# Result rows of expert slots: four homes chosen by the kind of slot, in place of two

## The chip, the cores and the metric

The kernel runs on one core of one Trainium2 chip. The metric is the device time of one execution in microseconds (us), as the median of several runs.

## What is computed

The input is 8 sequences of 512 rows of 256 numbers (4096 tokens). The reference adds three things: the input, a gated linear scan along each sequence, and a mixture of experts on the normalised rows. The change is in the last one:

```python
scores = jax.nn.sigmoid(xf @ Wg.T + bg + bias)
top_scores, top_idx = jax.lax.top_k(scores, TOP_K)      # 2 of 8 experts for each token
h = jax.nn.gelu(jnp.einsum('td,ehd->teh', xf, W1) + b1, approximate=False)   # 256 -> 1024
eo = jnp.einsum('teh,edh->ted', h, W2) + b2                                  # 1024 -> 256
combined = jnp.einsum('ted,te->td', eo, weights)
shared = jax.nn.gelu(xf @ Ws1.T + bs1, approximate=False) @ Ws2.T + bs2
```

The kernel computes an expert only for the tokens that chose it: 8192 pairs of token and expert, sorted into lists.

## The kernel before

**Two parts.** The first part runs over the 8 sequences: projections, scan, shared expert, routing, and the store of a base result to `out`. It ends near 275 us. The second part works through 43 slots. A slot is a run of list entries that belong to one expert, of 256 rows (28 of them, "large"), 128 rows (8) or 64 rows (7). The tables of constants fix the order: slots 0 to 13 are large, slot 14 has 128 rows, then come six blocks of large, 64-row, large, 128-row (slots 15 to 38), and at the end large, large, 64-row, 128-row (39 to 42). `order(n)` (line 89) makes the description of slot n. `s.u` is n modulo 2, `s.c` is n modulo 4, `s.kth` counts the slots of the same size before it, `s.added` is the value of the semaphore `add_out[s.u]` once all adds of the slots of this parity up to n have landed. `ahead(n, c)` (line 84) is the same for large slots inside a hardware loop, where n is a register's value.

**A slot's way through the engines.** The order is written out by hand, engine by engine.
- SP loads the slot's list of rows, its list of places and weights (`slot_adds`), its parameters and its second bias row. `adds_list(s, s2)` waits until the adds of slot n-2 have landed, then loads the list of slot n+2 (line 380). SP also copies 1 MB of weights for each 64-row slot (line 423), since those slots keep their weights apart.
- POOL gathers the rows from memory by index (line 557), four slots ahead.
- PE turns the rows (line 1375). In a large slot it turns those of slot n+2 at its fifth step, in a 128-row slot at its first one. Then it runs the first layer (lines 1297 for large, 1333 for small slots) three steps ahead of the second layer (1305, 1356).
- ACT applies the gelu (line 656), DVE splits the result into a high and a low half-precision part (lines 930 and 931), and PE's second layer reads these.
- In slot n DVE also writes, into the home of the slot's result, the weighted bias rows (`bias_rows`, line 1159, its instruction at 1168): in a large slot behind the sixth of eight splits, in a small slot behind the fourth of four. In slot n+1 DVE adds the weighted PSUM result to that home (`result`, line 1175, its instruction at 1188). For a 64-row slot the result is turned back in between.
- POOL then adds the home's rows to `out` by index (`scatter_add`, line 561, its instruction at 570), one DMA per 128-row tile. It first waits for the adds of slot n-1 to land, because two slots can add to the same row of `out`.

**The homes.** `y_sb` (line 182) has two homes of 512 columns in the scratch tile `arena`, used in turn by s.u. Before it writes bias rows, DVE waits until the home is free, which is when the adds of slot n-2 have landed:

```python
if not isinstance(s.n, int) or s.n >= 2:
    dve.wait_ge(add_out[s.u], s.added - 16 * s.tiles)
    dve.wait_ge(y_ok, s.n + S_A + 1)
```

Columns 4096 to 5120 of `arena` hold the base result of a sequence in the first part. In the second part 4096 to 4608 hold two of the four bias rows, and 4608 to 5120 are unused.

Of the kernel before, what the change touches and what calls it, by code (L numbers as in the profile page):

```python
# [29 lines left out]
ALU, ACT, AX = mybir.AluOpType, mybir.ActivationFunctionType, mybir.AxisListType  # L30
# [3 lines left out]
SEQS, SEQ, D, H, E = 8, 512, 256, 1024, 8  # L34
# [3 lines left out]
ROWS, MID, LOW = 256, 128, 64  # L38
NA, NB, NC = 28, 8, 7
SLOTS = NA + NB + NC  # L40
FIRST = NA // 2
# [20 lines left out]
EV_A, H_A, S_A = SEQS * EVENTS, SEQS * KH, 2 * SEQS  # L62
# [26 lines left out]
def order(n):  # L89

    if not 0 <= n < SLOTS:
        return None
    past = SIZES[:n]
    dmas = [16 * max(r // P, 1) for r in SIZES[:n + 1]]
    return Slot(n, n, SIZES[n], past.count(SIZES[n]), sum(UNITS[r] for r in past), sum(dmas[n % DEEP::DEEP]),
                sum(dmas[n % 2::2]))


class Tally:


# [22 lines left out]
def layer(nc, x, w1, w2, gates, b1, b2, gbias, sbias, out):  # L124
    ctx = ExitStack()
    with ctx:
        def sb(name, shape, dt):
            return ctx.enter_context(nc.sbuf_tensor(name, shape, dt))

        def sem(name):  # L130
            return ctx.enter_context(nc.semaphore(name))
# [12 lines left out]
        arena = sb("arena", [P, 7680], F32)  # L144
# [34 lines left out]
        spare = arena[:, 0:512].bitcast(U32)  # L179
        zeros = arena[:, 512:1024]  # L180
        b2rows = [b2row[0], b2row[1], arena[:, 4096:4096 + D], arena[:, 4096 + D:4096 + 2 * D]]
        y_sb = [arena[:, 2048 + i * 512:2560 + i * 512] for i in range(2)]
        low_w1, low_w2, mid_w1 = (h[:, :].bitcast(F16) for h in (stage[0], stage[1], arena[:, 5120:7168]))
        late = arena[:, 7168 + KD * LOW:7168 + KD * LOW + 256]
        factors = [small[:, 200 + 2 * i:202 + 2 * i] for i in range(2)]
# [91 lines left out]
        hhl_ok, y_ps, y_ok = sem("hhl_ok"), sem("y_ps"), sem("y_ok")  # L277
# [12 lines left out]
        add_out = [sem(f"add_out{i}") for i in range(2)]  # L290
# [173 lines left out]
        def _(pool):  # L464
            own = Tally(pool, pool_own)
# [95 lines left out]
            def scatter_add(s):  # L561

                if s.n:
                    pool.wait_ge(add_out[1 - s.u], order(s.n - 1).added)
                for t in range(s.tiles):
                    if t < s.tiles - 1:
                        pool.wait_ge(add_ok, s.kth + 1)
                    else:
                        pool.wait_ge(y_ok, S_A + s.n + 1 + 2)
                    pool.indirect_dma_start(  # L570
                        out, bass.IndirectOffsetOnAxis(ap=slot_adds[s.c][0:s.parts, t, 0:1], axis=0),
                        y_sb[s.u][0:s.parts, t * D:(t + 1) * D], None, compute_op=ALU.add).then_inc(add_out[s.u], 16)

            pool.wait_ge(xhl_out, 16 * SEQS)
            pool.wait_ge(ev_ps, EVENTS * (SEQS - 1))
# [2 lines left out]
            for n in range(SLOTS):  # L578
                if n + DEEP < SLOTS:
                    gather(order(n + DEEP))  # L580
                if n == 0:
                    pool.wait_ge(o_out, 16 * SEQS)
                scatter_add(order(n))
# [214 lines left out]
        def _(dve):  # L798
            own = Tally(dve, dve_own)
            V = nc.vector  # L800
# [358 lines left out]
            def bias_rows(s):  # L1159

                dve.wait_ge(b2_in[s.c], (s.n - s.c) * 4 + 16)
                dve.wait_ge(adds_list_in[s.c], (s.n - s.c) * 4 + 16)
                if not isinstance(s.n, int) or s.n >= 2:
                    dve.wait_ge(add_out[s.u], s.added - 16 * s.tiles)
                    dve.wait_ge(y_ok, s.n + S_A + 1)
                r, weight = s.parts, slot_adds[s.c][:, :, :].bitcast(F32)
                for t in range(s.tiles):
                    own.mark(V.scalar_tensor_tensor(out=y_sb[s.u][0:r, t * D:(t + 1) * D], in0=b2rows[s.c][0:r, :],
                                                    scalar=weight[0:r, t, 1:2], in1=bs2[0:r, :], op0=ALU.mult,
                                                    op1=ALU.add))  # L1170
                if s.rows != LOW:
                    own.mark(V.tensor_scalar(factors[s.u][:, 0:s.tiles], weight[:, 0:s.tiles, 1], par[s.c][:, 2:3], None,
                                             ALU.mult))

            def result(s):

                if s.rows == LOW:
                    dve.wait_ge(yT_ps, s.kth + 1)
                else:
                    dve.wait_ge(y_ps, s.unit + s.units + H_A + RING)  # L1180
                own.settle()
                for t in range(s.tiles):
                    r, c = s.parts, slice(t * D, (t + 1) * D)
                    if s.rows == LOW:
                        src, factor = ps_l[0:r, 0:D], slot_adds[s.c][0:r, 0, 1:2].bitcast(F32)
                    else:
                        src, factor = ps_y[s.u][:, c], factors[s.u][:, t:t + 1]
                    V.scalar_tensor_tensor(out=y_sb[s.u][0:r, c], in0=src, scalar=factor, in1=y_sb[s.u][0:r, c],  # L1188
                                           op0=ALU.mult, op1=ALU.add).then_inc(add_ok if t < s.tiles - 1 else y_ok, 1)

            def slot(s, back, late=(), first=False):

                for j in range(KH):
                    split_h(s, j, first)
                    if j == 0 and back is not None and back.rows == LOW:
                        turn(back)
                    if j == 1 and back is not None and back.rows != LOW:
                        result(back)
                    if j == 2 and back is not None and back.rows == LOW:
                        result(back)  # L1200
                    if j in late:
                        late_tables(late[j])
                    if j == 5:
                        bias_rows(s)

            def small_slot(s, back):

                for k in range(s.units):
                    split_h(s, k)
                    if k == 0 and back.rows == LOW:  # L1210
                        turn(back)
                    if k == 1:
                        result(back)
                    if k == 3:
                        bias_rows(s)
# [299 lines left out]
```

## Time and profile before

| | us |
|---|---|
| median of 3 runs (lowest, highest) | 672.48 (672.28, 672.95) |
| the profiled execution, its own time | 667.34 |
| its span, first to last instruction | 665.2 |
| mean granted clock of TensorE | 0.997 of full |

The profile shows one execution. PE is TensorE's matmuls, DVE VectorE, ACT ScalarE, POOL GpSimd, SP SyncE. "idle before <-releaser" is the time in which an engine stood before an instruction, and what ended that wait. A pair such as "arena L1168 <- DMA out" means: line 1168, which writes the arena, waited for a DMA that writes `out`. Busy time of a matmul is modelled, and some matmul records can be missing.

### The profile page before, as it was taken

How to read it: one execution, taken by the hardware profiler on the slowest of the kernel's cores; microseconds unless marked ns; L12 is line 12 of the kernel's file. 1: busy time of each engine (PE TensorE's matmuls, PEld its weight loads, DVE VectorE, ACT ScalarE, POOL GpSimd, SP SyncE). 2: the span in 40 equal slices, each digit the busy share in tenths (PEclk: the TensorE clock that was granted, in tenths of full speed). 3: DMA queues.
4: the chain of work that ended last, by engine and by line, in shares of the span. 5: the costliest groups of instructions: out<-in, count | busy, mean ns of one | idle time of the engine just before them, and what ended most of it. 6: DMA issues, size and time to landing. Idle time of an engine off the chain costs nothing.

```text
span 665.2 us, 19468 instructions
## 1 busy us (share of the span) xinstructions
PE 633.9 (95%) x6090; PEld 499.6 (75%) x6091; DVE 535.0 (80%) x1422; ACT 413.7 (62%) x703; POOL 279.3 (42%) x263
## 2 busy tenths in 40 slices
PE   4799999999999999999999999999999999999994
PEld 3365757575656665788888888999989998989883
DVE  4889898999999989887767677777777877787774
ACT  6997886969696966444445444556555554555552
POOL 3132323324242535345454545344545554545423
PEclk9999999999999999999999999999999999999998
DMA  7516345352526142333333254445656665666622
GB/s 243 211 40 184 96 128 112 111 138 83 168 75 199 33 100 68 106 75 59 64 53 68 49 127 116 121 112 138 188 162 161 186 152 167 168 162 192 189 40 29
DMA packets 69455, 81.02 MB, mean 122 GB/s; under 512 B 25684, under 2 KB 61460, under 8 KB 66568
## 3 DMA queue, kind: packets, MB, share of 16 engines
q1 hardware_dynamic: 54264, 62.35, 30.3%
q0 software_dynamic: 15120, 17.77, 15.4%
q8 instruction: 39, 0.64, 0.4%
q14 instruction: 32, 0.26, 0.2%
HBM read 38.66 MB, written 18.10 MB: 85 GB/s over the span
## 4 chain that ended last, share of the span: by engine, by line
PE 77%; DVE 8%; issue 5%; DMA 4%; ACT 3%; POOL 1%; POOLq 0%; SPq 0%; DVEq 0%; ACTq 0%
PE bank L1305 29%; PE bank L1297 29%; PE bank L1285 7%; PE bank L1356 4%; PE bank L1333 4%; DMA out<-arena,slot_adds 3%; PE bank L1375 2%; DVE arena L931 1%; DVE arena L930 1%; DVE W L837 1%; PE bank L1276 1%; DMA arena<-in_gates 1%; PE bank L1241 1%; ACT arena L656 1%; POOL out L570 1%
## 5 line engine op out<-in xcount | busy, mean ns | idle before, releaser
L1305 PE MATMUL bank<-W,arena 128*128 (+1 forms) x2112 | 276.9, 273 | 8.4 <-DVE arena L931 8.4
L1297 PE MATMUL bank<-rows,W 128*128 128x256 f16 (+1 forms) x1728 | 272.6, 296 | 2.3 <-issue 1.1
L656 ACT ACTIVATE arena<-bank,par 128x256 f32<-128x256 f32 (+2 forms) x344 | 169.6, 518 | 147.5 <-PE bank L1297 126.1
L1305 PEld LDWEIGHTS bank<-W,arena 128*128 128x128 f16 x2112 | 201.3, 98 | 44.8 <-issue 8.3
L1297 PEld LDWEIGHTS bank<-rows,W 128*128 (+1 forms) x1728 | 164.5, 98 | 56.5 <-issue 4.7
L570 POOL DMA_INDIRECT out<-arena,slot_adds x71 | 117.7, 1658 | 139.9 <-DVE arena L1188 76.3
L930 DVE TENSOR_SCALAR arena<-arena,par 128x256 f16<-128x256 f32 (+1 forms) x284 | 101.5, 357 | 52.3 <-ACT arena L656 47.4
L931 DVE SCALAR_TENSOR_TENSOR arena<-arena,par 128x256 f16<-128x256 f32 (+1 forms) x284 | 134.0, 472 | 10.0
L508 POOL DMA_INDIRECT lists<-entry,place x64 | 69.4, 1084 | 119.0 <-ACT arena L638 64.6
L1285 PE MATMUL bank<-rows,W 128*128 128x512 f16 x288 | 63.7, 379 | 0.0
L662 ACT ACTIVATE rows<-bank 128x1024 f16<-128x1024 f16 (+2 forms) x43 | 36.1, 840 | 36.3 <-PE bank L1375 35.9
L645 ACT ACTIVATE arena<-bank,PT 128x512 f32<-128x512 f32 x64 | 49.3, 772 | 10.2 <-DVE arena L931 10.2
L638 ACT ACTIVATE arena<-bank,small 128x512 f32<-128x512 f32 x48 | 36.6, 771 | 26.4 <-PE bank L1285 26.0
L557 POOL DMA_INDIRECT arena<-xhl_rows,slot_rows x34 | 34.8, 1023 | 40.4 <-ACT arena L656 34.7
L557 POOL DMA_INDIRECT rows<-xhl_rows,slot_rows x37 | 38.4, 1039 | 31.2 <-ACT arena L656 14.8
L1285 PEld LDWEIGHTS bank<-rows,W 128*128 128x128 f16 x288 | 27.5, 98 | 31.6
L931 DVE SCALAR_TENSOR_TENSOR arena<-arena,PT 128x512 f16<-128x512 f32 x64 | 48.2, 753 | 2.3
L837 DVE SCALAR_TENSOR_TENSOR W<-stage,small,W 128x1024 f16<-128x1024 f32 (+1 forms) x32 | 40.0, 1278 | 0.8 <-ACT W L612 0.8
L930 DVE TENSOR_SCALAR arena<-arena,PT 128x512 f16<-128x512 f32 x64 | 31.5, 492 | 8.0 <-PE bank L1305 6.2
L612 ACT ACTIVATE W<-stage,small 128x1024 f32 (+1 forms) x32 | 36.5, 1143 | 0.0
L601 ACT ACTIVATE W<-stage 128x1024 f32 (+1 forms) x32 | 33.5, 1047 | 0.0
L1188 DVE SCALAR_TENSOR_TENSOR arena<-bank,small,arena 128x256 f32<-128x256 f32 x64 | 28.4, 480 | 6.0 <-PE bank L1356 3.6
(186 smaller groups left out, 549.6 us busy)
## 6 DMA issues: line engine op xcount, KB each, us to landing
stage<-in_w SPq DMA_DIRECT2D x32, 512.0 KB, 4.7
stage<-W SPq DMA_DIRECT2D x14, 1024.0 KB, 5.5
arena<-W SPq DMA_DIRECT2D x8, 1024.0 KB, 5.6
arena<-in_x SPq DMA_DIRECT2D x8, 512.0 KB, 5.5
xhl_rows<-W SPq DMA_DIRECT2D x8, 512.0 KB, 4.5
out<-arena SPq DMA_DIRECT2D x8, 512.0 KB, 5.7
b2row<-in_b SPq DMA_DIRECT2D x22, 128.0 KB, 3.4
arena<-in_b SPq DMA_DIRECT2D x21, 128.0 KB, 3.7
```

The lines of the kernel that those rows point to most:

```text
L508: pool.indirect_dma_start(list_dram, bass.IndirectOffsetOnAxis(ap=place[u][:, c:c + 1], axis=0), entry[u][:, 2 * c:2 * c + 2], None).then_ ...
L557: pool.indirect_dma_start(xg[s.c][0:s.parts, t, :], None, xhl_dram, bass.IndirectOffsetOnAxis(ap=slot_rows[s.c][0:s.parts, t, 0:1], axis=0 ...
L570: pool.indirect_dma_start(out, bass.IndirectOffsetOnAxis(ap=slot_adds[s.c][0:s.parts, t, 0:1], axis=0), y_sb[s.u][0:s.parts, t * D:(t + 1) ...
L638: A((sg[ch], tv[ch], dec)[g], ps_e[(2 * u + i) % RING][:, :], ACT.Tanh, bias=sbt[:, 2 * g + ch:2 * g + ch + 1], scale=(a_half, a_gate, a_h ...
L645: A(h32w[i % WIDE], ps_e[(2 * u + PROJ + i) % RING][:, :], ACT.Gelu, bias=PT[:, 0, 4 + i:5 + i], scale=PT[:, 0, 0:1]).then_inc(ev_act, 1)
L656: ins = A(h32[k][:, c], ps_e[k][:, c], ACT.Gelu, bias=p[:, 4 + e * i + jj:5 + e * i + jj], scale=p[:, 0:1])
L837: ins = V.scalar_tensor_tensor(out=W[:, bass.ds(o + HALF, HALF // 2)], in0=landing(n, l)[:, part * HALF // 2:(part + 1) * HALF // 2], scal ...
L930: seq(V.tensor_scalar(hi, v, p[:, 1:2], None, ALU.mult))
L931: V.scalar_tensor_tensor(out=lo, in0=v, scalar=p[:, 1:2], in1=hi, op0=ALU.mult, op1=ALU.subtract).then_inc(hhl_ok, 1)
L1285: ins = T.matmul(ps_e[(2 * u + i) % RING][:, :], gw[:, wp, c, o:o + P], xT[u][:, 2 * xp + c, :], start=n == 0, stop=n == 3 * KD - 1)
L1297: ins = T.matmul(bank_, weights(w, wp * HALF + c * H + j * P, P), rhs[:, 2 * xp + c, :], start=n == 0, stop=n == 3 * KD - 1)
L1305: ins = T.matmul(banks[t // 2][:, (t % 2) * D:(t % 2 + 1) * D], h[:, hp, t * P:(t + 1) * P], weights(w, (2 + wp) * HALF + j * D, D), start ...
```

## The change

Slots below 14 keep the two homes by parity. From slot 14 on, the home goes by the slot's size: large slots have homes 0 and 1 in turn, by their count; 128-row slots have home 2 and 64-row slots home 3, of 256 columns each, at 4608 and 4864 of `arena`. The wait ahead of the bias rows now names the slot that had the same home last (`preceding`).

```diff
@@ -96,6 +96,16 @@
                 sum(dmas[n % 2::2]))
 
 
+def shares(s):
+
+    return s.u if not isinstance(s.n, int) or s.n < FIRST else s.kth % 2 if s.rows == ROWS else 2 + (s.rows == LOW)
+
+
+def preceding(s):
+
+    return next((order(n) for n in range(s.n - 1, -1, -1) if shares(order(n)) == shares(s)), None)
+
+
 class Tally:
 
 
@@ -179,7 +189,7 @@
         spare = arena[:, 0:512].bitcast(U32)
         zeros = arena[:, 512:1024]
         b2rows = [b2row[0], b2row[1], arena[:, 4096:4096 + D], arena[:, 4096 + D:4096 + 2 * D]]
-        y_sb = [arena[:, 2048 + i * 512:2560 + i * 512] for i in range(2)]
+        y_sb = [arena[:, a:b] for a, b in ((2048, 2560), (2560, 3072), (4608, 4608 + D), (4608 + D, 5120))]
         low_w1, low_w2, mid_w1 = (h[:, :].bitcast(F16) for h in (stage[0], stage[1], arena[:, 5120:7168]))
         late = arena[:, 7168 + KD * LOW:7168 + KD * LOW + 256]
         factors = [small[:, 200 + 2 * i:202 + 2 * i] for i in range(2)]
@@ -569,7 +579,7 @@
                         pool.wait_ge(y_ok, S_A + s.n + 1 + 2)
                     pool.indirect_dma_start(
                         out, bass.IndirectOffsetOnAxis(ap=slot_adds[s.c][0:s.parts, t, 0:1], axis=0),
-                        y_sb[s.u][0:s.parts, t * D:(t + 1) * D], None, compute_op=ALU.add).then_inc(add_out[s.u], 16)
+                        y_sb[shares(s)][0:s.parts, t * D:(t + 1) * D], None, compute_op=ALU.add).then_inc(add_out[s.u], 16)
 
             pool.wait_ge(xhl_out, 16 * SEQS)
             pool.wait_ge(ev_ps, EVENTS * (SEQS - 1))
@@ -1160,12 +1170,16 @@
 
                 dve.wait_ge(b2_in[s.c], (s.n - s.c) * 4 + 16)
                 dve.wait_ge(adds_list_in[s.c], (s.n - s.c) * 4 + 16)
-                if not isinstance(s.n, int) or s.n >= 2:
+                if not isinstance(s.n, int):
                     dve.wait_ge(add_out[s.u], s.added - 16 * s.tiles)
                     dve.wait_ge(y_ok, s.n + S_A + 1)
+                elif preceding(s) is not None:
+                    p = preceding(s)
+                    dve.wait_ge(add_out[p.u], p.added)
+                    dve.wait_ge(y_ok, S_A + p.n + 1 + 2)
                 r, weight = s.parts, slot_adds[s.c][:, :, :].bitcast(F32)
                 for t in range(s.tiles):
-                    own.mark(V.scalar_tensor_tensor(out=y_sb[s.u][0:r, t * D:(t + 1) * D], in0=b2rows[s.c][0:r, :],
+                    own.mark(V.scalar_tensor_tensor(out=y_sb[shares(s)][0:r, t * D:(t + 1) * D], in0=b2rows[s.c][0:r, :],
                                                     scalar=weight[0:r, t, 1:2], in1=bs2[0:r, :], op0=ALU.mult,
                                                     op1=ALU.add))
                 if s.rows != LOW:
@@ -1185,7 +1199,7 @@
                         src, factor = ps_l[0:r, 0:D], slot_adds[s.c][0:r, 0, 1:2].bitcast(F32)
                     else:
                         src, factor = ps_y[s.u][:, c], factors[s.u][:, t:t + 1]
-                    V.scalar_tensor_tensor(out=y_sb[s.u][0:r, c], in0=src, scalar=factor, in1=y_sb[s.u][0:r, c],
+                    V.scalar_tensor_tensor(out=y_sb[shares(s)][0:r, c], in0=src, scalar=factor, in1=y_sb[shares(s)][0:r, c],
                                            op0=ALU.mult, op1=ALU.add).then_inc(add_ok if t < s.tiles - 1 else y_ok, 1)
 
             def slot(s, back, late=(), first=False):
```

## Rows read from the trace of the kernel before

**Rows 1.** First part of the page: busy time, share of the span, instructions.

```profile
PE 633.9 (95%) x6090; PEld 499.6 (75%) x6091; DVE 535.0 (80%) x1422; ACT 413.7 (62%) x703; POOL 279.3 (42%) x263
```

**Rows 2.** Waits: us in total, times, longest; the second from 410 us on.

```profile
DVE arena L1168 <- DMA out<-arena,slot_adds: 11.3, 7, 3.0
...
PE bank L1305 <- DVE arena L931: 3.0, 3, 1.5
```

**Rows 3.** Chain that ended last, 470 to 565 us: start, us, what.

```profile
483.95 7.21 DMA out<-arena,slot_adds
...
546.60 8.06 DMA out<-arena,slot_adds
```

**Rows 4.** Timeline, DVE, bias rows that waited: start, us, instruction, idle before.

```profile
459.47 0.88 DVE L1168 SCALAR_TENSOR_TENSOR arena<-b2row,slot_adds,bs 128x256 f32<-128x256 f32 x2 [1.18 <-DMA out<-arena,slot_adds]
...
491.36 0.92 DVE L1168 SCALAR_TENSOR_TENSOR arena<-b2row,slot_adds,bs 128x256 f32<-128x256 f32 x2 [2.20 <-DMA out<-arena,slot_adds]
...
521.79 0.93 DVE L1168 SCALAR_TENSOR_TENSOR arena<-b2row,slot_adds,bs 128x256 f32<-128x256 f32 x2 [0.86 <-DMA out<-arena,slot_adds]
...
537.04 0.93 DVE L1168 SCALAR_TENSOR_TENSOR arena<-arena,slot_adds,bs 128x256 f32<-128x256 f32 x2 [0.26 <-DMA out<-arena,slot_adds]
...
554.85 0.93 DVE L1168 SCALAR_TENSOR_TENSOR arena<-b2row,slot_adds,bs 128x256 f32<-128x256 f32 x2 [3.05 <-DMA out<-arena,slot_adds]
...
585.89 0.93 DVE L1168 SCALAR_TENSOR_TENSOR arena<-b2row,slot_adds,bs 128x256 f32<-128x256 f32 x2 [1.50 <-DMA out<-arena,slot_adds]
...
617.73 0.93 DVE L1168 SCALAR_TENSOR_TENSOR arena<-b2row,slot_adds,bs 128x256 f32<-128x256 f32 x2 [2.26 <-DMA out<-arena,slot_adds]
```

**Rows 5.** Timeline, PE, the row turns in and behind slots 21, 25, 29, 33, 37.

```profile
490.06 0.61 PE L1375 MATMUL bank<-ident,arena 128*128 128x128 f16 x8
...
496.76 0.29 PE L1375 MATMUL bank<-ident,rows 64*128 64x64 f16 x4
...
521.83 0.61 PE L1375 MATMUL bank<-ident,arena 128*128 128x128 f16 x8
...
527.67 0.29 PE L1375 MATMUL bank<-ident,rows 64*128 64x64 f16 x4
...
552.71 0.61 PE L1375 MATMUL bank<-ident,arena 128*128 128x128 f16 x8
...
560.26 0.29 PE L1375 MATMUL bank<-ident,rows 64*128 64x64 f16 x4
...
585.29 0.61 PE L1375 MATMUL bank<-ident,arena 128*128 128x128 f16 x8
...
591.29 0.29 PE L1375 MATMUL bank<-ident,rows 64*128 64x64 f16 x4
...
616.33 0.61 PE L1375 MATMUL bank<-ident,arena 128*128 128x128 f16 x8
...
623.07 0.61 PE L1375 MATMUL bank<-ident,rows 128*128 128x128 f16 x8
```

**Rows 6.** Timeline, SP's and POOL's DMA issues around the stall of slot 29.

```profile
538.19 0.34 SPq L380 DMA_DIRECT2D slot_adds<-lists  x1
...
547.21 0.50 SPq L423 DMA_DIRECT2D stage<-W  x1
...
548.51 0.97 POOL L557 DMA_INDIRECT rows<-xhl_rows,slot_rows  x1 [0.30 <-issue]
...
554.93 1.43 POOL L570 DMA_INDIRECT out<-arena,slot_adds  x1 [5.46 <-DMA out<-arena,slot_adds]
...
560.79 1.03 POOL L557 DMA_INDIRECT rows<-xhl_rows,slot_rows  x1 [3.11 <-ACT arena L656]
```

**Rows 7.** Line 930 on DVE: all of it (ns min/median/max), and one beside POOL.

```profile
L930 DVE TENSOR_SCALAR arena<-arena,par x284: 276/347/672, 274.5 to 655.0; 128x256 f16<-128x256 f32 x128, 128x128 f16<-128x128 f32 x14
...
547.19 0.62 DVE L930 TENSOR_SCALAR arena<-arena,par 128x256 f16<-128x256 f32 x1
```

## The prediction

> **What bounds the kernel now.** I read the page's first part, then the list of waits, then the timelines of DVE and PE from slot 14 on, then those of POOL and SP around one stall. PE is busy for 95% of the span and DVE for 80% [rows 1], so only time in which PE stands still is to be had. In the list of waits the change touches one entry: DVE, ahead of the bias rows of a slot (line 1168), waits seven times for a scatter-add to land, 11.3 us in all [rows 2]. PE is held by DVE's second half of the hidden split (line 931) three times, 3.0 us [rows 2]. The reader should see that these are one story. In the chain of waits two pieces "DMA out<-arena,slot_adds" of 7.21 and 8.06 us stand between a scatter-add's issue and the bias rows [rows 3].
>
> The seven stalls are 1.18, 2.20, 0.86, 0.26, 3.05, 1.50 and 2.26 us [rows 4]. From slot 15 on the slots run in blocks of four (large, 64-row, large, 128-row). Six stalls are in the large slot after a 64-row one (17, 21, 25, 29, 33, 37), because the 64-row slot is short: little time passes between the result of slot n-2 and the bias rows of slot n. The 0.26 is in slot 27.
>
> **What a stall costs PE.** DVE's stall is not PE's loss, so I measured that apart. PE turns the rows of slot n+2 at fixed places of its own program: in the large slot after a 64-row one, ahead of the stall's effect, and at the start of the next (128-row) slot, behind it. The instructions between are the same in every block. The distance is 527.67 - 521.83 = 5.84 us around slot 25; around slot 17 it is the same. It is 496.76 - 490.06 = 6.70, 560.26 - 552.71 = 7.55, 591.29 - 585.29 = 6.00 and 623.07 - 616.33 = 6.74 us around slots 21, 29, 33 and 37 [rows 5]. So PE lost 0.86, 1.71, 0.16 and 0.90 us, in sum 3.63. Against the stalls of the same slots, 2.20, 3.05, 1.50 and 2.26 [rows 4], each loss is the stall less 1.34 to 1.36 us. That is the lead that DVE has over PE at this place; it also says why the stalls of 1.18, 0.86 and 0.26 cost nothing. PE's 3.0 us of idle [rows 2] is most of the 3.63; I take the rest for PE and its feeder ACT getting back into step.
>
> **The change, part by part.**
> 1. *Homes.* From slot 14 on, large slots use homes 0 and 1 in turn by their count, 128-row slots home 2, 64-row slots home 3. Homes 2 and 3 are each one tile of 256 columns at 4608 and 4864 of the arena. That is behind the two bias rows kept at 4096 to 4608, in the space of the shared result, whose store is waited for before the first scatter-add. No instruction is added, and the addresses change no shape: cost nothing.
> 2. *The wait ahead of the bias rows.* Before: all adds of the slots of the same parity up to n-2 have landed. After: those up to the slot that had the same home last, which is n-4 in the blocks (n-3 for slots 15 and 40, n-5 for 41, none for 14 and 16). The adds of n-4 were out before those of n-2 were issued, since POOL waits for each slot's adds ahead of the next slot's. So for slot 29 the new wait was met well before the stall began at 554.85 - 3.05 = 551.80 [rows 4], and all seven stalls go. Behind DVE's wait stood the last splits of the slot, and behind those PE's second layer: this is the 3.63 us.
> 3. *Waits that stay.* The same function waits for the slot's list and bias row. For slot 29 SP issued the list at 538.19 [rows 6], 13.6 us ahead of the time asked. The longest transfer shown took 8.06 us [rows 3], so a list of 2 KB is no new stall: cost nothing. SP still waits for the adds of n-2 before it loads the list of n+2, so SP does not get faster; nor does POOL, whose 64-row add waits 5.46 us for the same landing [rows 6]. These stand still while PE, DVE and ACT move up, by up to 1.71 us a block. What could be late next is behind them on these queues. POOL's gather after that add waits another 3.11 us for ACT [rows 6]: it has that much in hand, more than 1.71. The gather for slot 32 goes out at 548.51 and PE turns it at 560.26 [rows 6, 5], 11.75 us later and 10.0 after the change. Both are covered; cost nothing. If the cover were gone, the price would be at most the 1.71 us again in each block.
> 4. *First fourteen slots.* There the new expression gives the old numbers (n-2): nothing.
> 5. *The end.* From the result of slot 40 on, the last adds follow each other in series; none of the seven waits lies there. The whole end moves up: nothing gained or lost.
>
> Sum: -3.63 us against the profiled execution, 667.34 us with a span of 665.2. The median of the runs is 672.48, 5.14 us more than that execution. I take the same difference from it: 672.48 - 3.63 = 668.85, say **668.8 us**.
>
> The unknown term is how late the adds land where nothing records them. The adds share the DMA engines with a 1 MB copy of weights, issued at 547.21, 0.6 us behind the add of 8.06 us [rows 6, 3]. With every landing 0.5 us earlier PE's losses (stall less 0.5 less 1.34) are 0.36, 1.21 and 0.42, together 2.0. With every landing 0.5 later they are 0.34, 1.36, 0.02, 2.21, 0.66 and 1.42, together 6.0. I take the recorded 3.6 and keep 2.0 to 6.0, that is 666.5 to 670.5.
>
> The row for such a landing is 8.06 us from issue [rows 3]. The Trainium skill, DMA: Bandwidth & Descriptors, section on the anatomy of one DMA on the SWDGE path, fits a transfer as 2.0 us plus its bytes over 436 GB/s: an estimate of 2.3 us for one of these 128 KB adds. By that fit there would be no stall and nothing to gain; the trace disagrees for transfers beside others.
>
> **Rivals.**
> *A, the forecast:* the stalls go, PE gets 3.6 us back. For it: four independent pairs of stall and loss that obey one slack, and lists and gathers with room.
> *B, nothing measurable:* in the timed runs landings come 1 us earlier, so that only slot 29 loses anything (3.05 - 1 - 1.34 = 0.7 us; time 671.8), or a wait that is met at the same landing takes the old one's place (672.5). Against: the runs are slower than the profiled execution, not faster, and no other consumer of that landing is near PE.
> *C, slower:* POOL's issue holds DVE up. During the old stall DVE stood idle exactly while POOL was about to issue the 64-row add (1.43 us) and a gather (1.03) [rows 6]; now DVE works there. If DVE stood for both, it would be 2.46 us in each of the six slots, less 1.34 of lead: 1.12 x 6 = 6.7 us lost where 3.63 were, 672.5 + 3.1 = 675.6. It decides from a hold-up of 1.34 + 3.63/6 = 1.95 us a slot. Against: a DVE split at 547.19, right beside an issue of POOL, took 0.62 us where the median is 0.347 [rows 7]. That is 0.27 us for one instruction, inside the lead even if it happened four times in a block.
> The Trainium skill, SBUF — State Buffer, section Who interferes with whom, has the rule for this: a DVE instruction in a 2-port mode and a GpSimd one exclude each other for the whole instruction. The 0.62 agrees that there is something, not with the full length of POOL's issue.
> *D, more than forecast:* part of the 5.14 us by which the runs exceed the profiled execution are these very stalls. With landings 1 us later the losses are 0.84, 1.86, 0.52, 2.71, 1.16 and 1.92, together 9.0 us: 663.5. Nothing in the trace places the 5.14, so this is open.
> *E, it does not do what it says:* a home shared by mistake would leave a wait on n-2. By the order of sizes each class comes back after four slots, so I give it next to nothing and count it with B.
>
> **How the numbers follow.** A 0.75, D 0.07, B with E 0.13, C 0.05. A measurement of this kernel tells from no change what is over 0.2%, 1.35 us. A from its low bound up and D are faster: 0.82; same 0.13; slower 0.05. The range holds all of A (666.5 to 670.5), part of D below it and the near side of B above it: 665.0 to 671.2.
>
> **What would show it.** In the changed kernel's profile the wait "DVE arena L1168 <- DMA out" (the line moves by some ten) is gone, not moved. The distance from the row turn in slot 29 to the next is 5.84 us, as in all blocks. POOL's waits for landings stay. PE's busy time stays at 634 us while the span falls to about 661.6. I am wrong if DVE waits in the bias rows for a list, if PE shows new waits for gathered rows, if the distances shrink but others grow, or if DVE's splits beside POOL's issues take over 1 us.

## The result and the profile after

| | before | after |
|---|---|---|
| median (lowest to highest), 5 runs each | 672.48 (672.24 to 673.17) | 668.82 (667.78 to 670.13) |
| ratio of the times, 95% interval | | 0.9944 (0.9932 to 0.9955) |
| profiled execution, own time | 667.34 | 668.82 |
| its span | 665.2 | 667.0 |

The changed kernel is 3.7 us faster (672.48 - 668.82), where 3.6 was forecast. The last line of the table is the surprise: by the two profiled spans it would be 1.8 us *slower*. Both readings had to be explained before the forecast could be called right for its reason.

First part of the page of the changed kernel; the engines do the work they did before [rows 1]:

```profile
span 667.0 us, 19466 instructions
## 1 busy us (share of the span) xinstructions
PE 635.1 (95%) x6090; PEld 499.4 (75%) x6091; DVE 534.3 (80%) x1422; ACT 411.1 (62%) x703; POOL 281.7 (42%) x263
```

The wait at the bias rows (now line 1182) is in no list of waits any more, where it stood with 11.3 us [rows 2]. POOL still waits for landings, 44.2 us against 44.9 before, but DVE no longer stands behind these landings. In the chain that ended last, by engine, DMA is down to 1% from 4% before, and no scatter-add's landing [rows 3] is among its costly lines:

```profile
PE 76%; DVE 13%; issue 6%; ACT 3%; DMA 1%; POOLq 0%; DVEq 0%; SPq 0%; POOL 0%; ACTq 0%
```

PE's timeline, the row turns (now line 1389) in and behind slots 21, 25 and 29, to be held against [rows 5]:

```profile
482.11 0.39 PE L1389 MATMUL bank<-ident,arena 128*128 128x128 f16 x4
...
492.77 0.61 PE L1389 MATMUL bank<-ident,arena 128*128 128x128 f16 x8
498.61 0.29 PE L1389 MATMUL bank<-ident,rows 64*128 64x64 f16 x4
...
524.33 0.61 PE L1389 MATMUL bank<-ident,arena 128*128 128x128 f16 x8
530.18 0.29 PE L1389 MATMUL bank<-ident,rows 64*128 64x64 f16 x4
...
545.05 0.39 PE L1389 MATMUL bank<-ident,arena 128*128 128x128 f16 x4
...
555.95 0.61 PE L1389 MATMUL bank<-ident,arena 128*128 128x128 f16 x8
561.79 0.29 PE L1389 MATMUL bank<-ident,rows 64*128 64x64 f16 x4
```

Behind the large slots the distance is 498.61 - 492.77 = 5.84 us, and 5.85 and 5.84 at the next two, where it was 6.70, 5.84 and 7.55. That part came as forecast. But ahead of them, from the turn in the 64-row slot to the one in the large slot, it is 555.95 - 545.05 = 10.90 us, where the kernel before had 10.16. In all six blocks it is 0.50 to 0.78 us above the same distance before. PE's timeline shows why, in the middle of a run of equal matmuls:

```profile
548.09 0.51 PE L1370 MATMUL bank<-arena,stage 128*128 128x64 f16 x10
549.12 0.22 PE L1370 MATMUL bank<-arena,stage 128*128 128x64 f16 x2 [0.53 <-issue]
```

Twelve matmuls that follow each other without any wait on a semaphore are cut after the tenth, by 0.53 us with no releaser ("issue"). Each of the six blocks has such a pause: two inside this third run of twelve, four in the first-layer matmuls (line 1311) right behind it. The profile of before has none. Either the change brings them, or the two profiles come from different circumstances.

Part of the difference of the spans arises ahead of slot 14, from which on the change acts. These are the same row turn in PE's timelines, of the kernel before and of the changed one:

```profile
425.46 0.39 PE L1375 MATMUL bank<-ident,arena 128*128 128x128 f16 x4
```
```profile
427.17 0.39 PE L1389 MATMUL bank<-ident,arena 128*128 128x128 f16 x4
```

Here the second profile is already 1.7 us behind. With 3.8 us more in the six 64-row slots and 3.7 us less at the large slots it ends 1.8 us behind (1.7 + 3.8 - 3.7), which is the difference of the spans. The 1.7 us can't come from the wait that was changed.

### The profile page after: what moved, and what is told of

It reads as the page before. It is cut to its first block, busy times and chain, and to the rows that moved or that the text cites. A ratio compares the mean times of both kernels' runs of the same rounds, so it can differ in the third digit from the quotient of the medians.

```text
span 667.0 us, 19466 instructions
## 1 busy us (share of the span) xinstructions
PE 635.1 (95%) x6090; PEld 499.4 (75%) x6091; DVE 534.3 (80%) x1422; ACT 411.1 (62%) x703; POOL 281.7 (42%) x263
## 4 chain that ended last, share of the span: by engine, by line
PE 76%; DVE 13%; issue 6%; ACT 3%; DMA 1%; POOLq 0%; DVEq 0%; SPq 0%; POOL 0%; ACTq 0%
PE bank L1319 29%; PE bank L1311 28%; PE bank L1299 5%; PE bank L1370 5%; PE bank L1347 5%; PE bank L1389 2%; DVE W L847 2%; DVE arena L941 2%; DVE arena L940 2%; DMA arena<-in_gates 1%; PE bank L1290 1%; DVE arena L880 1%; DVE arena L874 1%; PE bank L1255 1%; ACT W L622 1%
## 5 line engine op out<-in xcount | busy, mean ns | idle before, releaser
L666 ACT ACTIVATE arena<-bank,par 128x256 f32<-128x256 f32 (+2 forms) x344 | 167.7, 518 | 149.9 <-PE bank L1311 126.0
```

Source lines behind the costliest of these rows:

```text
L666: ins = A(h32[k][:, c], ps_e[k][:, c], ACT.Gelu, bias=p[:, 4 + e * i + jj:5 + e * i + jj], scale=p[:, 0:1])
```

## The experiments

Three sets of four kernels. The kernels of a set ran on one chip, and each set on another chip. "Ratio" is to the kernel before on the same chip; its median was 666.43, 673.46 and 666.10 us in the three sets.

### First set: is the gain this wait, and on every chip?

**The kernel before, no edit.** Expected:

> The kernel before, unchanged. Open after the result: its profiled execution took 667.34 us, its timed ones 672.2 to 673.2. Theory A (the seven waits are worth 3.6 us in every execution): median 672.5, and a profile of such an execution shows the distances between row turns around slots 21, 29, 33 and 37 above 5.84 us by 3.6 in sum. Theory D (the shown execution was a lucky one; typical ones lose more to the same waits): the losses sum to 5 to 9 us. Theory F (typical executions lose 3 to 4 us in 64-row slots to pauses of PE that have no releaser, as in the profile of the changed kernel): the distance from the row turn in a 64-row slot to the one in the large slot after it is 10.7 to 10.9 us instead of 10.16.

Measured: 666.56 us, ratio 0.9999 (0.9991 to 1.0008), span 664.2. **The changed kernel, no edit.** Expected:

> The changed kernel, unchanged. All theories: median 668.8, ratio 0.994 to 0.995. A and D: distances of 5.84 us behind the large slots that follow a 64-row one. F: in the 64-row slots 10.7 to 10.9 us again; if they are a property of single executions and not of this kernel, 10.16 can show up.

Measured: 663.23 us, ratio 0.9951 (0.9937 to 0.9965), span 661.3. DVE's bias rows and PE's row turns of the kernel before, on this chip:

```profile
491.47 0.93 DVE L1168 SCALAR_TENSOR_TENSOR arena<-b2row,slot_adds,bs 128x256 f32<-128x256 f32 x2 [2.56 <-DMA out<-arena,slot_adds]
...
522.68 0.93 DVE L1168 SCALAR_TENSOR_TENSOR arena<-b2row,slot_adds,bs 128x256 f32<-128x256 f32 x2 [1.65 <-DMA out<-arena,slot_adds]
```
```profile
489.82 0.61 PE L1375 MATMUL bank<-ident,arena 128*128 128x128 f16 x8
496.88 0.29 PE L1375 MATMUL bank<-ident,rows 64*128 64x64 f16 x4
...
521.95 0.61 PE L1375 MATMUL bank<-ident,arena 128*128 128x128 f16 x8
528.09 0.29 PE L1375 MATMUL bank<-ident,rows 64*128 64x64 f16 x4
```

Slot 21 loses 496.88 - 489.82 - 5.84 = 1.22 us to a stall of 2.56, slot 25 loses 0.30 to one of 1.65: the stall less 1.34 and 1.35. The stalls are not the same ones as in the profile of before (slot 25 had 0.86 and lost nothing), the lead is. Slots 29 and 33 lose 1.09 and 0.45, for stalls of 2.35 and 1.80 (1.26 and 1.35 less). The losses of this execution sum to 1.22 + 0.30 + 1.09 + 0.45 = 3.06 us, and the spans differ by 664.2 - 661.3 = 2.9. The medians differ by 3.2, for about 0.3 us of the gain lies outside the span. In every run of a kernel that has the old wait in all slots, the time is 2.1 to 2.2 us more than the span; in every run of the others it is 1.8 to 1.9 us more. What those 0.3 us are stays open. The changed kernel has 5.84 us at each place and 10.16 to 10.26 in the blocks' other part: no pauses. So the change alone does not bring the pauses.

**Homes without the shorter wait.**

```diff
-                if not isinstance(s.n, int):
+                if not isinstance(s.n, int) or s.n >= 2:
                     dve.wait_ge(add_out[s.u], s.added - 16 * s.tiles)
```

> The four homes with the old wait (the adds of slot n-2). A and D: as slow as before, 672.5, DVE's seven waits are back. A rival by which the addresses or the program's changed layout bring the gain: 668.8.

Measured: 666.62 us, ratio 1.0003 (0.9991 to 1.0014). DVE's waits are back, one of them longer than any seen before:

```profile
618.09 0.93 DVE L1182 SCALAR_TENSOR_TENSOR arena<-b2row,slot_adds,bs 128x256 f32<-128x256 f32 x2 [3.11 <-DMA out<-arena,slot_adds]
```

This stall is in slot 37, and PE lost 1.81 us there; the losses sum to 4.1 us, and the span is 4.1 above the changed kernel's (665.4 - 661.3). The new addresses alone are worth nothing; the wait is everything.

**The old wait in four slots.**

```diff
-                if not isinstance(s.n, int):
+                if not isinstance(s.n, int) or s.n in (21, 29, 33, 37):
                     dve.wait_ge(add_out[s.u], s.added - 16 * s.tiles)
```

> The changed kernel with the old wait put back in slots 21, 29, 33 and 37 alone, those where the stall exceeded DVE's lead of 1.34 us in the profile of before. A: the three relieved stalls (slots 17, 25, 27) were worth nothing, so 672.5 as before. D: typical executions lose in 17 and 25 too, so 671 to 672, between the two kernels.

Measured: 665.82 us, ratio 0.9989 (0.9977 to 1.0002), 0.6 us below before and not clear of it. As a ratio that is where D put it (671 to 672 of 672.5), and the interval just reaches A's 1.0; neither is excluded. Which slots exceed the lead changes from execution to execution, so on this chip slot 25 can be worth something, as the profile of the kernel before had shown (0.30). The four slots of the list carry most of the gain: with them waiting, 2.6 of the 3.2 us are gone again (665.82 - 663.23).

### Second set: how large is the lead, and what part of the change is needed?

**Three homes.** 128-row and 64-row slots share home 2.

```diff
-    return s.u if not isinstance(s.n, int) or s.n < FIRST else s.kth % 2 if s.rows == ROWS else 2 + (s.rows == LOW)
+    return s.u if not isinstance(s.n, int) or s.n < FIRST else s.kth % 2 if s.rows == ROWS else 2
```

> 128-row and 64-row slots share home 2; large slots keep homes 0 and 1 by their count. The small slots then wait again for the adds of slot n-2. A: large slots wait for n-4 still, and no small slot waited in the profile of before, so this is as fast as four homes: ratio to before 0.995. A rival by which each kind needs its own home: back towards 1.0.

Measured: 672.99 us, ratio 0.9986 (0.9970 to 1.0002): not the 0.995. DVE's and POOL's timelines of its end show a term that I had overlooked when I wrote the variant:

```profile
660.15 1.67 POOL L580 DMA_INDIRECT out<-arena,slot_adds  x1 [2.48 <-DMA out<-arena,slot_adds]
...
663.83 0.48 DVE L1182 SCALAR_TENSOR_TENSOR arena<-arena,slot_adds,bs 128x256 f32<-128x256 f32 x1 [3.32 <-DMA out<-arena,slot_adds]
...
665.79 1.56 POOL L580 DMA_INDIRECT out<-arena,slot_adds  x1 [3.98 <-DVE arena L1202]
```

Slots 41 and 42 are the only small slots that are neighbours. Sharing a home, slot 42's bias rows wait for slot 41's add to land, the last add goes out 5.64 us after it in place of 3.49 in the kernel before (659.22 - 655.73), and nothing follows to hide it. Behind the large slots PE kept 5.84 us (5.75 at slot 37). The third set has a variant without this wait, to see whether it was the cause.

This profile shows something else that the account here leaves open. In two of its 64-row slots the distance is 12.26 and 12.24 us, where pauses alone make about 10.9; in both, PE waits 0.98 and 0.92 us for DVE's line 941. The next two variants have two such waits each in these slots (0.30 to 1.07 us). The changed kernel's three profiles and that of the late bias rows below have none. The kernel before has no profile on this chip, so whether it pays this too is not known.

**Three and six more instructions on DVE** ahead of the bias rows of the six large slots that follow a 64-row one, on the changed kernel. They write unused scratch; this is with six (twice three), and three has one round:

```diff
+                if isinstance(s.n, int) and s.n in (17, 21, 25, 29, 33, 37):
+                    for i in range(2):
+                        own.settle()
+                        for to in (rt[:, 0:256], rt[:, 256:512], late):
+                            own.mark(V.scalar_tensor_tensor(out=to, in0=bs2[:, :], scalar=par[s.c][:, 2:3], in1=bs2[:, :],
+                                                            op0=ALU.mult, op1=ALU.add))
```

> Four homes, and ahead of the bias rows of slots 17, 21, 25, 29, 33 and 37 three more VectorE instructions of 256 columns, about 0.40 us apart (0.88 us for two in the profile), so 1.2 to 1.3 us. A (DVE leads PE by about 1.34 us there): no loss, ratio still 0.995; the distances stay at 5.84 us. Rival (no lead, DVE's work counts in full): 6 x 1.25 = 7.5 us more, ratio 1.006.

> The same with six instructions, 2.5 to 2.6 us. A: each of the six slots loses that less 1.34, about 1.2 us, 7 us in all: 4 us slower than before, ratio 1.005 to 1.006. Rival without a lead: 15 us, ratio 1.018.

Measured with three: 670.93 us, ratio 0.9963 (0.9948 to 0.9978), and distances of 5.84 and 5.85 us (5.75 at slot 37). Measured with six: 677.03 us, ratio 1.0049 (1.0031 to 1.0067). DVE's and PE's timelines at slot 21, with six:

```profile
493.64 0.88 DVE L1184 SCALAR_TENSOR_TENSOR rt<-bs,par 128x256 f32<-128x256 f32 x2
494.43 0.48 DVE L1184 SCALAR_TENSOR_TENSOR arena<-bs,par 128x256 f32<-128x256 f32 x1
494.95 0.88 DVE L1184 SCALAR_TENSOR_TENSOR rt<-bs,par 128x256 f32<-128x256 f32 x2
495.75 0.48 DVE L1184 SCALAR_TENSOR_TENSOR arena<-bs,par 128x256 f32<-128x256 f32 x1
496.14 0.88 DVE L1188 SCALAR_TENSOR_TENSOR arena<-b2row,slot_adds,bs 128x256 f32<-128x256 f32 x2
```
```profile
498.07 0.84 PE L1325 MATMUL bank<-W,arena 128*128 x6 [0.95 <-DVE arena L941]
```

The six take 496.14 - 493.64 = 2.50 us. The distance at this slot is 6.98 us, so it loses 1.14, and the lead by this is 1.36; over the six slots it is 1.36 to 1.47. Three take 1.19 us by the same reading and lose nothing. In all six slots the losses are 1.10, 1.14, 1.07, 1.03, 1.03 and 1.05, 6.4 us; the two times differ by 677.03 - 670.93 = 6.1. No DMA plays a part here: the lead is DVE's own, and a held-up DVE costs nearly the same whatever holds it.

**Two homes, bias rows later.** The kernel before with the bias rows of those six slots behind the eighth split.

```diff
-                    if j == 5:
+                    if j == (7 if isinstance(s.n, int) and s.n in (17, 21, 25, 29, 33, 37) else 5):
                         bias_rows(s)
```

> The kernel before, two homes and the old wait, but in slots 17, 21, 25, 29, 33 and 37 the bias rows stand behind the eighth split in place of the sixth, 2.6 us later. A: stalls of up to 2.6 us vanish and 3.05 shrinks to 0.4, so this gets the gain without new homes: ratio 0.995 to 0.996. Rival (the bias rows' own 1.1 us now stand where DVE has less lead, just ahead of the next slot): ratio 0.997 to 1.000.

Measured: 672.18 us, ratio 0.9984 (0.9969 to 0.9999), in the rival's range. Yet its profile looks like A's: two short waits are left (the first is slot 21, the second slot 29), and all distances behind the large slots are unstretched (5.84 or 5.85 us, 5.75 at slot 37).

```profile
494.49 0.92 DVE L1168 SCALAR_TENSOR_TENSOR arena<-b2row,slot_adds,bs 128x256 f32<-128x256 f32 x2 [0.43 <-DMA out<-arena,slot_adds]
...
558.06 0.93 DVE L1168 SCALAR_TENSOR_TENSOR arena<-b2row,slot_adds,bs 128x256 f32<-128x256 f32 x2 [0.78 <-DMA out<-arena,slot_adds]
```

On this chip every one of the four kernels shows the pauses of 64-row slots, this one too, whose instructions on PE are those of the kernel before:

```profile
549.60 0.71 PE L1297 MATMUL bank<-rows,W 128*128 128x256 f16 x5 [0.42 <-issue]
...
581.10 0.19 PE L1356 MATMUL bank<-arena,stage 128*128 128x64 f16 x1 [0.53 <-issue]
```

So they come and go with the chip. Its times spread over 669.39 to 674.13, and its profiled execution (span 667.3) is the fastest of them; one profile does not say what the others lost.

### Third set: the mended variants, and before and after on one more chip

**The kernel before, no edit,** and **the changed kernel, no edit:**

> The kernel before once more, for its profile on the chip of this set. If the set lands on a chip where the 64-row slots show pauses of PE without a releaser (10.7 to 10.9 us from row turn to row turn, as in the last set), they are there too for this kernel: a property of the chip, not of the change. Theory A: its losses around slots 21 to 37 sum to 3 to 4 us and equal, within 0.5 us, the difference of its span to that of the changed kernel. Rival: on such a chip the losses are smaller, since the pauses in the 64-row slot lengthen the time between the result of slot n-2 and the bias rows of slot n, so the gain is smaller there.

> The changed kernel on the same chip: ratio 0.994 to 0.996, distances of 5.84 us.

Measured: 665.89 us, ratio 1.0003 (0.9993 to 1.0014), span 663.6; and 662.92 us, ratio 0.9953 (0.9937 to 0.9970), span 661.1. A stall that was 0.26 us in [rows 4] is long here, in the kernel before, at slot 27 behind a 128-row slot:

```profile
539.38 0.93 DVE L1168 SCALAR_TENSOR_TENSOR arena<-arena,slot_adds,bs 128x256 f32<-128x256 f32 x2 [2.23 <-DMA out<-arena,slot_adds]
```

PE lost 0.84 us there (541.37 us, 0.65 idle, and 5.00 us between two row turns that else are 4.16 apart), which gives a lead of 1.39. The losses sum to 0.45 + 1.09 + 0.84 + 0.11 = 2.5 us, and so do the spans: 663.6 - 661.1. This chip had no pauses, so whether the kernel before loses less on a chip with pauses was not seen in a profile. The times say: not much less, 3.7 us in the first comparison, whose changed kernel had them. In the second set the changed kernel itself was not run; with three more instructions on DVE it was 2.5 us below before (673.46 - 670.93).

PE's row turns in the changed kernel on this chip, around slots 29 and 37:

```profile
541.27 0.39 PE L1389 MATMUL bank<-ident,arena 128*128 128x128 f16 x4
...
551.43 0.61 PE L1389 MATMUL bank<-ident,arena 128*128 128x128 f16 x8
557.27 0.29 PE L1389 MATMUL bank<-ident,rows 64*128 64x64 f16 x4
...
613.32 0.61 PE L1389 MATMUL bank<-ident,arena 128*128 128x128 f16 x8
619.06 0.61 PE L1389 MATMUL bank<-ident,rows 128*128 128x128 f16 x8
```

**Three homes, the last slot in home 0.**

```diff
-    return s.u if not isinstance(s.n, int) or s.n < FIRST else s.kth % 2 if s.rows == ROWS else 2 + (s.rows == LOW)
+    return s.u if not isinstance(s.n, int) or s.n < FIRST else s.kth % 2 if s.rows == ROWS else 2 * (s.n < SLOTS - 1)
```

> Three homes with the last slot in home 0, so that slot 42 doesn't wait for the adds of slot 41, its neighbour, as it did in r5 (3.32 us). A: as fast as four homes, within 0.2% of r10. Rival (small slots need homes apart): slower than r10 by 1.5 us or more, as r5 was.

Measured: 663.32 us, ratio 0.9962 (0.9948 to 0.9976), span 661.1 as with four homes: within 0.1%. So the wait at the end was what the first three-home variant lost by. What is needed is one home off the turn of the large slots for the small ones, not two.

**The late bias rows again.**

> Two homes with the late bias rows. In r8 its profile showed no loss at the large slots, its time 0.9984 of before. If the delay removes the stall as a whole, it is within 0.1% of r10; if longer landings in other executions still reach through, or the bias rows' 1.1 us behind the last split cost, it stays 0.1 to 0.3% slower than r10.

Measured: 663.36 us, ratio 0.9962 (0.9949 to 0.9976), 0.44 us above four homes. On this chip moving one step of DVE's program by two splits brings nearly all of the gain, with two homes and no change of a wait. Its profile has two waits left, 0.75 and 0.37 us, and all distances behind the large slots are unstretched. Why the same kernel got only 0.9984 on the chip of the second set stays open. Longer landings in its other executions would do it, and so would the bias rows' own time standing in a place with less lead; neither was tried there.

No version beat the changed kernel.

## Why the prediction was right, point by point

*What bounds the kernel, and what a stall costs.* Right, and the step that carried the number. "The stall less 1.34 to 1.36 us" held, with a wider spread, for the stalls of four other executions with the old wait in all or four slots (1.26 to 1.39), and for a load that has nothing to do with DMA (1.36 to 1.47). One point was slightly off: at slot 37 the undisturbed distance is 619.06 - 613.32 = 5.74, not 5.84. The profile of before lost 0.99 there, at a lead of 1.27, and 3.72 in sum rather than 3.63.

*The size.* On the two chips without pauses, the gain is 3.2 us (666.43 - 663.23) and 3.2 us (666.10 - 662.92), and the losses read from single profiles of before are 3.1 and 2.5. The forecast of 3.6 is within the spread of what one execution loses (2.5 to 4.1, the last with four homes and the old wait). That the median came within 0.1 us of the forecast is luck: 3.6 was read from one execution of a kernel whose executions differ by over 1 us in this, and the 0.3 us outside the span were in no term.

*"I take the same difference from it."* The 5.14 us between the profiled execution and the runs were left unexplained, and the prediction survived this only because they are, by the times, in both kernels. In the changed kernel's profile they are seen: 3.8 us in the six 64-row slots, 0.5 to 0.8 us each, and 1.8 us ahead of slot 14 (427.17, against 425.35 for the same row turn in the first set). On the chips without pauses both kernels are about 6 us faster than in the first comparison: before 672.48 - 666.43 = 6.0, after 668.82 - 663.23 = 5.6. The profile of before matches those chips (667.34), not the one of its runs. So the two profiled spans, 665.2 and 667.0, can't be held against each other; that it was another chip is inferred, not recorded.

*Homes and addresses at nothing:* right, 1.0003 with the old wait. *Lists, bias rows and gathers at nothing:* right, line 1182 waits for nothing in any profile of the changed kernel, and PE waits for no DMA in them.

*Rival B* (nothing): refuted in three comparisons. *Rival C* (POOL's issue holds DVE up): refuted. Where a stall used to be, the distances are 5.84 us, and DVE's line 940 has a median of 347 to 348 ns and a maximum of 672 to 674 ns in the changed kernel's three profiles, against 347 and 672 before [rows 7]. The Trainium skill, SBUF — State Buffer, section Who interferes with whom, says of a GpSimd instruction and a DVE instruction in a 2-port mode that whichever issues first blocks the other for its whole length. In none of these profiles did a split take more than 0.33 us above the median (0.672 - 0.347), against 1.4 to 1.9 us for POOL's issues; whether a split ran in such a mode is not shown. *Rival D* (the 5.14 us are these very stalls): refuted, since the changed kernel, without the stalls, has them too.

*What would show it:* the wait gone, the distances of 5.84 and POOL's waits kept came true. The span of 661.6 did not come in the first profile (667.0), but did on the two chips without pauses (661.3 and 661.1). By one of its own signs of being wrong, "the distances shrink but others grow", the first profile spoke against the prediction; only the two later chips, without that growth, cleared it.

## What to carry to other kernels

Price a stall of a side engine by the path's own clockwork, not by its length: find two events of the bounding engine with a fixed program between them, one ahead and one behind, and subtract the undisturbed distance. Here only what exceeded about 1.35 us of lead counted, 2.5 to 4 of 10 to 12 us. Before two profiled spans are compared, see that each stands where its kernel's timed runs stand; a profile whose own time is outside the spread of the runs tells of mechanisms, not of totals. A buffer that turns by parity is freed late when short pieces of work lie between long ones. Giving the short ones a home of their own helped on every chip where it was tried; moving the waiting step later helped nearly as much on one chip and less on another.

## What was not expected of the hardware

- The same program shows, on some chips, pauses of PE without a releaser (0.2 to 0.5 us each) most of them in its densest stretch, the runs of twelve small weight loads and 64-column matmuls, or in the first-layer matmuls between and behind these runs. On others it shows none. All five profiles with them show them in four to six of the six 64-row slots, and all six slots are longer there; ACT has more such idle time in them too. These lines are from the lists of ACT's waits, first in the changed kernel's first profile, then on the chip of the third set.

```profile
ACT arena L666 <- issue: 6.8, 12, 0.8
...
ACT rows L672 <- issue: 3.6, 2, 2.0
```
```profile
ACT arena L666 <- issue: 2.3, 7, 0.6
```

Late instructions are a guess that fits "no releaser" on two engines; no run tested it. The two DMA queues that the page calls "instruction" don't decide it: they carry 39 and 32 or 33 packets in every profile, with pauses or without.

- The landing of the same scatter-add varies from execution to execution by more than a microsecond: slot 25 stalled 0.86, 1.65 and 1.11 us, slot 27 0.26 and 2.23, slot 37 2.26, 1.14 and 0.81, always in the kernel before. The slots that pay change; the sum went from 2.5 to 3.7 us.
